# Slices of the layer-0 FFN stage issued between the head pairs of the attention ahead of it, in a two-layer transformer on 8 cores

## What is computed

```
# layer 0
q, k = quat_norm(quat_linear(x, ..)), quat_norm(quat_linear(x, ..)); v = quat_linear(x, ..)
scores = q k^T / 8 + c ; attn = softmax(scores)          # 16 heads of 64, all 4096 keys
x = LN(x + quat_linear(attn v, oW, ob))
xd, wd = x and weight, quantized in blocks of 32 to an FP6 grid and scaled back
x = LN(x + xd @ wd.T + bias)
# layer 1
x = LN(x + windowed attention(x))                         # 16 heads, 2 key heads, window 256
x = LN(x + sigmoid(xr Wr) * (relu(xk Wk)^2 Wv))           # xr, xk mix each row with the row before
```

## Time and profile before

| | |
|---|---|
| median of 2 runs | 5492.57 us (5486.91 to 5498.23) |
| profiled execution | 5488.6 us, span of its slowest core 5487.1 us |
| spans of the cores | 5473.3 to 5487.1 us |
| PE / DVE / ACT busy | 2805.3 / 1687.1 / 1746.2 us |
| exponentials of layer 0 (L513) | 1536, 1384.0 us |
| PV matmuls (L537) | 9216, 476.8 us |

### The profile page before, as it was taken

The page is one execution under the profiler, slowest core; times in us unless marked ns, Lnnn a source line. Parts: engine busy times, 40 slices in busy tenths (PEclk is TensorE's granted clock), DMA queues, the critical chain, the costliest instruction groups (busy, mean ns, idle before and its releaser), DMA issues.

```text
span 5487.1 us, 63802 instructions; the slowest of 8 cores (5473.3 to 5487.1 us)
## 1 busy us (share of the span) xinstructions
PE 2805.3 (51%) x17954; PEld 1392.3 (25%) x17954; DVE 1687.1 (31%) x3698; ACT 1746.2 (32%) x2188; POOL 178.0 (3%) x339
## 2 busy tenths in 40 slices
PE   0255247777776501776777633433255554545434
PEld 0122113444343100443444411111133331212112
DVE  0477310000000145000000045565145443344444
ACT  0000006777775001767667711011023230010000
POOL 0011010000000100000000000000000000000000
PEclk9977576666666755555555566666655556777666
DMA  1322230000001310000000010000300002111000
GB/s 16 77 31 35 45 47 2 4 4 4 4 4 19 50 39 23 1 4 4 4 4 4 1 29 28 28 27 25 59 18 12 24 13 52 31 23 31 23 23 23
DMA packets 174640, 123.34 MB, mean 22 GB/s; under 512 B 106824, under 2 KB 157680, under 8 KB 174320
## 3 DMA queue, kind: packets, MB, share of 16 engines
q0 software_dynamic: 46864, 59.31, 6.4%
q1 hardware_dynamic: 127456, 59.95, 4.0%
HBM read 117.63 MB, written 23.59 MB: 26 GB/s over the span
## 4 chain that ended last, share of the span: by engine, by line
PE 31%; ACT 26%; DVE 20%; issue 9%; DMA 9%; SPq 2%; POOL 1%; DVEq 1%; ACTq 1%; PEldq 0%; POOLq 0%
ACT TE L513 21%; PE PALL L537 9%; PE PALL L461 3%; PE PALL L331 2%; PE PALL L1111 2%; PE PALL L502 2%; DMA TY<-XFF 2%; ACT TE L1087 2%; PE PALL L830 2%; PE PALL L1219 2%; PE PALL L1043 1%; PE PALL L1423 1%; PE PALL L1353 1%; DMA SMALL<-QBI 1%; PE PALL L1274 1%
## 5 line engine op out<-in xcount | busy, mean ns | idle before, releaser
L513 ACT ACTIVATE TE<-PALL,BIASB 128x768 bf16<-128x768 f32 x1536 | 1384.0, 901 | 752.6 <-PE PALL L502 615.7
L502 PE MATMUL PALL<-TY 64*128 64x384 bf16 x3072 | 876.9, 429 | 545.1 <-ACT TE L513 540.6
L502 PEld LDWEIGHTS PALL<-TY 64*128 64x128 bf16 x3072 | 302.6, 99 | 1086.5 <-issue 1023.1
L537 PE MATMUL PALL<-TY,TE 128*128 128x65 bf16 x9216 | 476.8, 234 | 0.0
L537 PEld LDWEIGHTS PALL<-TY,TE 128*128 128x128 bf16 x9216 | 465.2, 126 | 32.0 <-issue 32.0
L331 PE MATMUL PALL<-TY,TE 128*128 128x512 bf16 (+1 forms) x832 | 205.6, 413 | 372.3 <-DVE TE L297 208.2
L1087 ACT ACTIVATE TE<-PALL,BIASB 128x256 bf16<-128x256 f32 (+2 forms) x240 | 154.7, 645 | 501.4 <-PE PALL L1072 482.7
L549 DVE TENSOR_TENSOR PVAB<-PVAB,PALL 128x390 f32<-128x390 f32 x48 | 27.0, 562 | 924.2 <-PE PALL L537 885.7
L461 PE MATMUL PALL<-TE,TY 128*128 128x512 bf16 x512 | 150.3, 446 | 255.5 <-DMA TY<-XFF 255.5
L749 PE MATMUL PALL<-TE,TY 128*128 128x512 bf16 x288 | 105.0, 529 | 326.6 <-DVE TY L642 208.8
L544 DVE COPY PVAB<-PALL 128x390 f32<-128x390 f32 x48 | 27.1, 565 | 775.1 <-PE PALL L537 758.5
(11 more groups left out here) (186 smaller groups left out, 3031.2 us busy)
## 6 DMA issues: line engine op xcount, KB each, us to landing
TY<-XFF POOLq DMA_DIRECT2D x192, 128.0 KB, 4.9
TY<-XST POOLq DMA_DIRECT2D x18, 512.0 KB, 4.1
YOUT<-TE SPq DMA_DIRECT2D x18, 512.0 KB, 2.6
ATT<-TY SPq DMA_DIRECT2D x36, 128.0 KB, 1.8
Y2SP<-TY SPq DMA_DIRECT2D x18, 256.0 KB, 2.0
ATT<-TY SPq DMA_DIRECT2D x18, 256.0 KB, 2.3
TE<-Y2SP POOLq DMA_DIRECT2D x18, 256.0 KB, 3.2
TY<-QW SPq DMA_DIRECT2D x32, 128.0 KB, 2.3
```

The source lines that it names most:

```text
L502: t.matmul(o_, l_, r_, start=True, stop=True, tile_position=tp)),
L513: ss.activation(o_, i_, AF.Exp, bias=BIASB[:, 63:64], scale=0.125)),
L537: t.matmul(o_, l_, r_, start=s0, stop=False, skip_group_check=True)),
```

## The change

`emit_p1c` takes a `hook`, called after each head pair with `(3*qt - 1, 2)` and, behind the three ATT0 writes at the end of a query tile, with `(3*qt + 2, 4)`: the last slice that may be begun, and how many pieces may be emitted. For group 1 the hook is `p2_pump`, which emits the pieces f1, f2 and back of p2 in a fixed order of preference. What is left is emitted after attention. The definitions of p2's helpers move ahead of attention of group 1 unchanged, except that the spill of a slice now counts on a semaphore of its own, dy2, on which the readers of Y2SP wait.

```
-        def emit_p1c(g, ready, state, nsets=3):
+        def emit_p1c(g, ready, state, nsets=3, hook=None):
...
                             state["pva_free"] = ntok
+                    if hook:
+                        hook(3 * qt - 1, 2)
                 sp = None
...
                 state["atm_free"] = sp
+                if hook:
+                    hook(3 * qt + 2, 4)
...
-            p2s["spill"][sl] = sch.dma("y", "dsp", (lambda y, r0=128 * sl:
+            p2s["spill"][sl] = sch.dma("y", "dy2", (lambda y, r0=128 * sl:
...
-        p2_f1(0); p2_f2(0); p2_f1(1)
-        for sl in range(NSL):
-            p2_back(sl)
-            if sl + 1 < NSL:
-                p2_f2(sl + 1)
-            if sl + 2 < NSL:
-                p2_f1(sl + 2)
+        p2drv = {"nf1": 0, "nf2": 0, "nb": 0}
+
+        def p2_pump(avail, budget):
+            done = 0
+            while done < budget:
+                k = p2drv["nb"]
+                if (k < NSL and p2drv["nf2"] >= min(k + 1, NSL)
+                        and p2drv["nf1"] >= min(k + 2, NSL)):
+                    p2_back(k); p2drv["nb"] += 1; done += 1; continue
+                k = p2drv["nf2"]
+                if k < NSL and p2drv["nf1"] >= k + 1 and p2drv["nb"] >= k:
+                    p2_f2(k); p2drv["nf2"] += 1; done += 1; continue
+                k = p2drv["nf1"]
+                if k < NSL and k <= avail and p2drv["nb"] >= k - 1:
+                    p2_f1(k); p2drv["nf1"] += 1; done += 1; continue
+                break
+
+        st_p1c = emit_p1c(1, [v_done1], st_p1c, nsets=2, hook=p2_pump)
+        att0_done = st_p1c["atm_free"]
+        p2_pump(NSL, 10 ** 9)
+        tg1 = sch.op("t", lambda t: t.nop(), mark=True)
...
-                    w = [("dsp", sch.cnt["dsp"]), tp2_nop, p2v_last]
+                    w = [("dy2", 16 * NSL), tp2_nop, p2v_last]
...
-            w = [tp3_nop]
+            w = [tp3_nop, ("dy2", 16 * NSL)]
```

More of the change, by code:

```diff
@@ L32 @@
 ENGS = ("t", "v", "s", "g", "y")
-DMA_SEMS = ("da", "db", "dw0", "dw1", "dw2", "dw3", "dm", "dgm", "dsp", "dl0", "dl1", "dx0", "dx1", "dxa", "dxb", "dout")
+DMA_SEMS = ("da", "db", "dw0", "dw1", "dw2", "dw3", "dm", "dgm", "dsp", "dy2", "dl0", "dl1", "dx0", "dx1", "dxa", "dxb", "dout")
 class Sched:
@@ L873, in p2_back @@
                                        waits=[t2ap])
-        p2_f1(0); p2_f2(0); p2_f1(1)
-        for sl in range(NSL):
-            p2_back(sl)
-            if sl + 1 < NSL:
-                p2_f2(sl + 1)
-            if sl + 2 < NSL:
-                p2_f1(sl + 2)
-        p2v_last = p2s["ln2"][NSL - 1]
+        p2drv = {"nf1": 0, "nf2": 0, "nb": 0}
[17 more added lines that the diff above has]
+        tg1 = sch.op("t", lambda t: t.nop(), mark=True)
+        p2v_last = p2s["ln2"][NSL - 1]
+        if stage == "p1c":
+            for sl in range(NSL):
+                sch.dma("g", "dout", (lambda gg, sl_=sl: gg.dma_start(
+                    out=DBG[:, sl_ * 1024: (sl_ + 1) * 1024],
+                    in_=ATT0[128 * sl_:128 * sl_ + 128, :])),
+                    waits=[("dsp", sch.cnt["dsp"])])
+            sch.op("y", lambda y: y.wait_ge(sem_handles["dout"], sch.cnt["dout"]))
+            sch.emit(block, sem_handles)
+            stack.close()
+            return nc
         if stage == "p2":
@@ L888, in build_program @@
                     in_=Y2SP[128 * sl_:128 * sl_ + 128, :])),
-                    waits=[("dsp", sch.cnt["dsp"])])
+                    waits=[("dy2", 16 * NSL)])
             sch.op("y", lambda y: y.wait_ge(sem_handles["dout"], sch.cnt["dout"]))
```

## The result

| | before | after |
|---|---|---|
| median | 5494.5 us (34 runs) | 5505.4 us (35 runs) |
| ratio | | 1.0024, 95% interval 1.0013 to 1.0035 |
| profiled execution, slowest core | 5487.1 us | 5532.8 us (core 6; the other cores 5487.5 to 5523.2) |
| start of group 1's exponentials to the end of the last slice's last DVE instruction | 1687.7 us | 1702.4 us |
| ACT busy / PV matmuls busy in the whole span | 1746.2 / 476.8 us | 1746.2 / 453.4 us |

The change moves slices 0 to 13, and all of slice 14 but its back, into attention and gains nothing; the kernel is 11 us slower. The profiled execution began late: its core 6 runs the first exponential of group 0 at 869.7 us, where the same instruction starts at 837.5 on the core profiled before, and nothing of the change lies ahead of that.

What follows compares the result with a forecast made beforehand. Attention and slices were taken as chains with no engine full, a slice set by DVE with its waits. Hooks and tail added +47.9 us, the clock -20: +28 on 5488.6 gives 5517 us, range 5470 to 5570.

Steps and rivals of the forecast that it cites:

- after tile 0: Behind query tile 0, f1(0), f2(0), f1(1), back(0): ACT free 67.9 us after the last exponential, cost 63.3 us.
- D: Behind head pair 2, f2(3k+2): exponentials go on 17.3 us after the batch's last, cost 12.7 us.
- B: Behind head pair 0, back(3k), f2(3k+1): exponentials go on 33.1 us after the batch's last, cost 28.5 us.
- A: At a tile's end, f1(3k), back(3k-1), f2(3k), f1(3k+1): exponentials go on 65.2 us after the last, cost 60.6 us.
- C: Behind head pair 1, f1(3k+2), back(3k+1): ACT free 27.1 us after the batch's last exponential, cost 22.4 us.
- after the last exponential: Behind attention, f1(15), back(14), f2(15), f1(16), then slice 15's first copy to the last slice's end: 158.3 us.
- whole stretch: Start of group 1's attention to the last slice's end: grows from 1687.7 to some 1715 us, +28 us.
- The clock: Hooks break the slow rhythm of PV's matmuls at 19 head pairs: -20 us, two thirds of 31.
- the clock gives back all: Rival: every PV near 4.0 us, -62 in place of -20, 5474 us; chance 0.12.
- the clock takes more: Rival: matmuls, transposes and copies in hooks slowed by half clock, 63 us more, no PV gain, 5600 us; chance 0.09.
- Real overlap: Rival: ACT and PE don't stand for the slices' chains, each slice costs only busy time, 5235 us; chance 0.06.
- rival 3: Real overlap: 15 slices at 20 us plus 158 give 458 in place of 712, 5235 us; chance 0.06.

Runs made afterwards that it cites:

- e2: The changed kernel with the DMA transposes of f1(3k+1) issued at a tile's end ahead of back(3k-1)'s spill; 5488.3 us, 0.9981 of the kernel before.
- e5: The changed kernel with ACT's part of the slices left out (Squares, Ln, Exp, Abs); 5363.0 us, 0.9739 of the kernel before.
- e3: The changed kernel with no hook at a tile's end and budgets of 3, 3, 2, 2 behind the four head pairs; 5387.9 us, 0.9803 of the kernel before.
- e4: The changed kernel's pieces cut into single instructions with due steps in the batch, z2 in its own buffer; 5019.8 us, 0.9133 of the kernel before.

## Why the prediction was right

Predicted 5517 us and no measurable change, a little slower; measured 5505.4, ratio 1.0024. The order of the pieces came out as listed. The terms, as gaps in us:

| | predicted | measured |
|---|---|---|
| after tile 0 | 67.9 | 68.1 |
| tile 1, D and B | 17.3, 33.1 | 16.6, 34.2 |
| A | 65.2 | 65.0, 64.1, 63.4, 63.9 |
| B | 33.1 | 32.8, 33.1, 33.2, 33.2 |
| C | 27.1 | 23.6, 24.3, 23.6, 23.8 |
| D | 17.3 | 17.1, 16.6, 17.4, 17.1 |
| gap without a hook | 4.6, less a gain of 20 in all | 4.03 in the mean of 28 |
| after the last exponential | 158.3 | 157.5 |
| whole stretch | +28 | +14.7 |

- **A, B, D and the tail** hold within 2 us each, built from rows of before where the pieces stood beside other work. That agrees with the fixed order on each engine as the mechanism; e2 and e5 show for A and for B, C, D which engine holds them, and e3 that the same pieces cost less where none waits for fresh rows.
- **C was mis-sized**, by 3.3 us four times, 13 us. That equals the error of the whole stretch (+14.7 for +28) partly by luck: A's four gaps are 4.4 us shorter in all, and the gaps without a hook gained 15 to 16 us and not 20, and these two cancel. I gave f1 8.3 us from its first matmul to its second add, from a stretch in which PE had stood for 17.8 us. In C it comes right behind PV:

```profile
2803.14 4.68 PE L537 MATMUL PALL<-TY,TE 128*128 128x65 bf16 x96
2807.65 1.89 PE L738 MATMUL PALL<-TE,TY 128*128 128x512 bf16 x8
2809.47 0.50 PE L742 MATMUL PALL<-ROWR,ONER 1*128 1x512 f32 x1
2809.91 1.90 PE L738 MATMUL PALL<-TE,TY 128*128 128x512 bf16 x8
```

  Eight matmuls take 1.89 us in place of 3.57, the clock is up, and the adds end 5.5 us after the first matmul (2813.17), which is 2.8 us of it. Another 0.9 is that PE comes free 3.2 us after the last exponential and not 4.1, as PV is shorter (4.68 for 5.32 us). The row for a duration has to be taken from a place where PE was doing the same beforehand.
- **The clock** (-20 predicted). PV's matmuls in group 1 take 229.4 us where they took 252.8, 23 less; on the exponentials' side the 28 gaps without a hook are some 0.57 us shorter each, 16 us, and 3.6 us more lie in C's four gaps (the 0.9 above). The guess of two thirds was near; it was a guess.
- **Rivals.** That the clock gives back all (5474 us) is out: a PV is 4.78 us in the mean of group 1, not near 4.0. That the clock takes more (5600 us) is out: the matmuls in hooks ran at both levels as in the steady slices. In the first A the granted clock is 0.50 and 0.52 in the first eight matmuls of its two f1, and 1.00 in the second eight of the later one; in the first C it is 1.00 from f1's start. Real overlap (5235 us) is out for this order: no batch starts while a Square waits. e4 shows that the idle shares of the earlier trace rows were real and that the granularity and the placing of the pieces kept them shut: rival 3 priced the slices' work at 20 us a slice, and e4 paid 1028.7 - 976.1 = 52.6 us for 13 slices and more.

The Trainium skill ("TensorE: Matmul & The Clock Gate", Architectural detail) says that ScalarE and VectorE run first-in first-out. The trace is in line with it: in D, ACT stands with score tiles ready behind the Square and the Abs for 12 us, and e5, in which nothing but the Square and its like is gone, has 4.0 us there. It doesn't test it, and here the prediction went wrong: it said that without this rule the sum would be rival 3's. But `Sched.op` makes every ACT and DVE instruction wait for the one before it on its engine, so in these kernels the program itself keeps that order, whatever the engine would do. Neither the sum nor the result hangs on the rule.

Not tried: the same fine order for group 0 or for layer 1's stages, e2 and e3 together, and both halves of e4 undone at once, which would say whether 161 and 112 us add up.

## What to carry to other kernels

Issuing a stage's pieces between another's batches gains nothing if a piece is a chain over several engines: each engine reaches its part, waits for the others, and what stands behind waits too. All that was hidden here was the part of a piece that holds neither engine of the other stage (10.7 us of DVE per slice). Count, for each engine, how long it stands in the chain, and compare with the stage run alone; here 124 us were forecast against 114, and 120 measured. What pays is to put single instructions in the free part of a step, each behind its input by more than the input's latency, and DMAs that read back fresh rows a whole piece ahead of their use, in front of any DMA on the same queue that waits.

## What the runs showed of the hardware that I had not expected

- ACT goes over from a slice's instruction to an exponential and back at 0.1 us (in e4: 2805.61 + 1.06 + the accumulator read of 0.19, less their overlap of 0.1, then 2806.85), the same 0.1 us that lies between two exponentials. No table load stands in this stage, though Square, Abs, Ln and Exp mix.
- The same f1 takes 8.3 or 5.5 us from its first matmul to its last add by what PE did in the microseconds before, and a change that shortened A by 9.3 us (e2) lost about 2 of them in the next batch and B, with PV at 238.4 us for 229.4.
- Exponentials, DVE's 1024-wide instructions and the 512-column matmuls kept their durations when they ran side by side in e4: 0.901 and 1.22 us, and 0.38 to 0.63 us by the clock, as before.
